# Query projection of a fused attention and feed-forward kernel, as seven half-size products per block instead of eight

## The chip, the cores and the metric

The kernel runs on one core of one Trainium2 chip. The metric is the device time of one launch in microseconds (us). Before the change it is 1665.83 us, the median of 3 runs (1663.76 to 1665.88).

## What is computed

Two layers, each a cross attention and a feed-forward stage, are applied to x of 32 x 64 = 2048 tokens with 512 features. The change is in the first attention, whose reference is:

```
q = (layernorm(x) @ wq).reshape(b, tq, HQ, D)      # HQ = 32 heads of D = 128; wq is 512 x 4096
k = (ctx @ wk).reshape(b, tk, HKV, D)              # HKV = 8; wk, wv are 512 x 1024
v = (ctx @ wv).reshape(b, tk, HKV, D)
scores = einsum('bqhd,bkhd->bhqk', q / sqrt(D), repeat(k, 4))
probs = softmax(scores, axis=-1)                   # 64 x 64 for each head and sequence
x = x + einsum('bhqk,bkhd->bqhd', probs, repeat(v, 4)).reshape(b, tq, HQ * D) @ wo
```

## The kernel before

Every matrix product works on pairs of float16 numbers: an operand is split into a high part (ScalarE casts) and a low part (VectorE subtracts), and three products are summed (high by high, high by low, low by high: `PASSES`).

A first part, the opening, loads x and the context, normalises x (VectorE computes the statistics, GpSimd writes `XN`), transposes both on TensorE and splits them into `XT` and `CT` in units of one PSUM bank. Then `attention0` loops over 8 groups; a group is one key head with its four query heads. Seven of the groups run as a hardware loop and the last is written out. Within a group there are four windows (t = 0 to 3), one for each block of 512 tokens.

TensorE's order in the window of block t is written by hand: scores of block t; the projections of the block after it, four query heads in turn, then the key; weighing of values of block t, pair 0 (it needs `PT`, the transposed probabilities, which come by DMA); the value projection of the next block; pair 1; the output projection of block t in four pieces, added into `X` by VectorE (`accumulate`). Each unit of a projection goes through one of two banks `pj`; ScalarE copies its high part (`high`), VectorE subtracts the low part (`low`), and then the bank is free again.

VectorE and ScalarE each have an order written by hand too. On VectorE: maximum and difference for both halves of the scores (`scores_less_max`), then for each half sums, the low part of a query head, and `normalise`; `low_probs` twice; the remaining low parts; `low_out`; `accumulate`. SyncE issues the DMA transposes of `EH` into `PT` once both high and both low halves are there. The kernel also prepares the fp8 weights of the feed-forward stage beside this: in window 1 and 2 ScalarE scales eight tiles, and in windows 2 and 3 it copies 1024 columns (`high_weights`), while GpSimd has two operations after each of windows 1 and 2, and nothing else in a group. In window 2 both ScalarE and VectorE split the next group's `WQ` and `WKV`, VectorE between the first and second `accumulate`.

## Time and profile before

| what | value |
|---|---|
| median of 3 runs | 1665.83 us (1663.76 to 1665.88) |
| profiled execution, span from first to last instruction | 1663.4 us |
| time outside the span (median less span) | 2.4 us |
| TensorE matmuls | busy 1510.4 us, 91% of the span |
| VectorE | busy 1273.3 us, 77% |
| ScalarE | busy 789.3 us, 47% |
| GpSimd | busy 289.0 us, 17% |
| bytes moved by DMA | 113.48 MB, 68 GB/s on average |

The profile was taken on one execution, and it gives a span only; its own time is taken as the span plus the 2.4 us around it. In the profile PE is TensorE, DVE is VectorE, ACT is ScalarE, POOL is GpSimd, SP is SyncE. Busy shares are averages over the stages; the first attention is the part from 56.8 to about 1011 us.

### The profile page before, as it was taken

To read this page: it belongs to the slowest core of one execution; us is meant where nothing else is said; L and a number is where in the kernel's file an instruction comes from. 1 tells how busy PE (TensorE), PEld (TensorE's weight loads), DVE (VectorE), ACT (ScalarE), POOL (GpSimd) and SP (SyncE) were. 2 spreads that over 40 slices of the span, in tenths; PEclk is the share of its full clock that TensorE was granted. 3 is DMA by queue.
4 is the path that set the end of the run, shared out by engine and by line. 5 is a ranking of instruction groups with operands and counts; after the bars stand their busy time and mean duration, and the time that the engine had idled before them with its cause. 6 is when DMAs were issued, how large, how long until landed. Compare 5 with 4: busy or idle time off the path is not lost. (4 is left out here: it accounts for less than half of the span.)

```text
span 1663.4 us, 29998 instructions
## 1 busy us (share of the span) xinstructions
PE 1510.4 (91%) x11382; PEld 803.7 (48%) x11398; DVE 1273.3 (77%) x2386; ACT 789.3 (47%) x1677; POOL 289.0 (17%) x249
## 2 busy tenths in 40 slices
PE   5799999999999999999999987799999998787695
PEld 4455455555555555555555543344444544344353
DVE  6577667667677667767776786899999986999777
ACT  3343433424334243342333332566777763888652
POOL 2001002001011011011011001111211103789620
PEclk7799999999999999999999998899999999899898
DMA  7031231321312212221312112122222350767402
GB/s 265 1 78 51 68 85 26 79 75 43 98 39 66 76 52 64 68 61 52 77 51 62 48 70 102 23 45 45 45 44 44 58 117 1 140 107 123 79 1 101
DMA packets 273838, 113.48 MB, mean 68 GB/s; under 512 B 239154, under 2 KB 255539, under 8 KB 273460
## 3 DMA queue, kind: packets, MB, share of 16 engines
q1 hardware_dynamic: 234820, 78.67, 21.6%
q10 hardware_dynamic: 38896, 33.03, 6.3%
q8 instruction: 94, 1.54, 0.4%
q14 instruction: 28, 0.23, 0.0%
HBM read 44.57 MB, written 11.53 MB: 34 GB/s over the span
## 5 line engine op out<-in xcount | busy, mean ns | idle before, releaser
L627 PE MATMUL xp<-WO,OT 128*128 128x512 f16 x1536 | 341.1, 382 | 5.6 <-DVE X L824 5.6
L585 PE MATMUL pj<-XT,WQ 128*128 128x512 f16 x1536 | 339.0, 381 | 6.4 <-PEq L379 6.4
L627 PEld LDWEIGHTS xp<-WO,OT 128*128 128x128 f16 x1536 | 148.2, 98 | 189.3 <-issue 18.4
L585 PEld LDWEIGHTS pj<-XT,WQ 128*128 128x128 f16 x1536 | 148.4, 98 | 182.3 <-DVE WKV L294 6.7
L705 ACT ACTIVATE E<-E 128x512 f32<-128x512 f32 x64 | 40.1, 627 | 329.0 <-DVE E L801 329.0
L824 DVE SCALAR_TENSOR_TENSOR X<-xp,X 128x512 f32<-128x512 f32 x128 | 88.2, 690 | 113.0 <-PE xp L627 112.0
L565 POOL TENSOR_TENSOR VW<-VW,XB 128x1024 f32<-128x1024 f32 x14 | 32.9, 2351 | 769.8 <-DVE VW L107 769.8
L1028 PE MATMUL db<-W0T,XD 128*128 128x448 f16 x768 | 162.2, 363 | 0.0
L1045 PE MATMUL eb<-W1T,DT 128*128 128x512 f16 x672 | 147.7, 380 | 4.2 <-ACT EB L1120 2.5
L766 DVE SCALAR_TENSOR_TENSOR QT<-pj,QT 128x512 f16<-128x512 f32 x128 | 88.0, 687 | 67.9 <-ACT QT L688 67.6
L1028 PEld LDWEIGHTS db<-W0T,XD 128*128 128x128 f16 x768 | 76.9, 100 | 74.7 <-issue 8.0
L688 ACT ACTIVATE QT<-pj 128x512 f16<-128x512 f32 x128 | 75.5, 590 | 71.1 <-PE pj L585 71.0
L1100 ACT ACTIVATE VD<-VD,dscale 128x128 f32<-128x128 f32 x224 | 68.7, 390 | 75.1 <-DVE VD L1202 75.1
L1045 PEld LDWEIGHTS eb<-W1T,DT 128*128 128x128 f16 x672 | 65.6, 98 | 78.7 <-DMA DT<-HL 1.1
L775 DVE TENSOR_TENSOR OT<-tv,OT 128x512 f16<-128x512 f32 x128 | 82.3, 684 | 13.8 <-ACT OT L697 11.1
L590 PE MATMUL pj<-WKV,CT 128*128 128x128 f16 x1536 | 91.3, 220 | 0.9 <-DVE QT L766 0.9
L585 PE MATMUL pj<-CT,WKV 128*128 128x512 f16 x384 | 88.2, 380 | 4.0 <-DVE QT L766 4.0
L590 PEld LDWEIGHTS pj<-WKV,CT 128*128 128x128 f16 x1536 | 85.9, 98 | 7.7 <-issue 6.3
L697 ACT ACTIVATE OT<-tv 128x512 f16<-128x512 f32 x128 | 69.3, 593 | 26.2 <-PE tv L616 26.2
L710 ACT ACTIVATE EH<-E 128x512 f16<-128x512 f32 x64 | 40.3, 630 | 84.5 <-DVE E L813 84.5
L1401 POOL TENSOR_TENSOR CT<-CT 128x512 f16<-128x512 f32 x64 | 72.6, 1159 | 16.9 <-ACT CT L1631 16.7
L1093 ACT ACTIVATE VD<-DB,drec 128x128 f32<-128x128 bf16 x224 | 67.2, 387 | 12.3 <-DVE drec L85 12.3
(236 smaller groups left out, 2427.0 us busy)
## 6 DMA issues: line engine op xcount, KB each, us to landing
W0T<-in_L_xattn_wq ACTq DMA_DIRECT2D x7, 1024.0 KB, 5.3
W0T<-in_L_xattn_wo ACTq DMA_DIRECT2D x7, 1024.0 KB, 5.0
CS<-in_ctx SPq DMA_DIRECT2D x4, 1024.0 KB, 10.1
X<-in_x SPq DMA_DIRECT2D x4, 1024.0 KB, 11.2
out<-X SPq DMA_DIRECT2D x8, 512.0 KB, 3.6
XB<-in_L_ffn_W ACTq DMA_DIRECT2D x28, 128.0 KB, 2.8
w0t<-XB ACTq DMA_DIRECT2D x7, 512.0 KB, 3.3
w1t<-W0T ACTq DMA_DIRECT2D x7, 512.0 KB, 3.8
```

Of the source, the lines that this page charges most:

```text
L585: last = pe.matmul(bank[:, :], w, src[:, b, k, tokens], start=n == 0, stop=n == 3 * KC - 1)
L590: last = pe.matmul(bank[:, i * P:(i + 1) * P], CT[:, a, k, own], WKV[:, b, k, 1, :], start=n == 0, stop=n == 3 * KC - 1)
L627: last = pe.matmul(xp[i % 2][:, :], OT[:, a, j, i * P:(i + 1) * P], WO[:, b, j, :], start=n == 0, stop=n == 3 * REP - 1)
L688: act.activation(QT[:, 0, :, u, :], q_bank(u), ACT.Copy, scale=UNSCALE).then_inc(S["pj_hi"], 1)
L697: act.activation(o_out(0, pair, h), o_bank(h), ACT.Copy).then_inc(S["ot_hi"], 1)
L766: dve.scalar_tensor_tensor(out=to[0], in0=q_bank(u), scalar=UNSCALE, in1=to[1], op0=ALU.mult, op1=ALU.subtract).then_inc(S["pj_lo"], 1)
L775: dve.tensor_tensor(o_out(1, pair, h), o_bank(h), o_out(0, pair, h), ALU.subtract).then_inc(S["ot_lo"], 1)
L824: dve.scalar_tensor_tensor(out=xt, in0=xp[i % 2][:, :], scalar=UNSCALE, in1=xt, op0=ALU.mult, op1=ALU.add).then_inc(S["x_acc"], 1)
L1028: last = pe.matmul(db[q][:, 0:NQ], XD[:, i[1] % 2, a, k, :], W0T[:, b, k, q * NQ:(q + 1) * NQ], start=False, stop=n == 3 * KC - 1)
L1045: last = pe.matmul(eb[:, :], DT[:, a, c, :], W1T[:, b, c, :], start=False, stop=c == IC - 1 and (a, b) == PASSES[-1])
L1100: last = act.activation(VD[:, r, c, :], VD[:, r, c, :], ACT.Copy, scale=ds_[:, r, c:c + 1])
L1401: pool.tensor_tensor(EH[:, 1, q, :], E[:, q, :, :].rearrange("p u n -> p (u n)"), EH[:, 0, q, :], ALU.subtract).then_inc(S["e_lo"], 1)
```

## The change

The four query heads of a group are computed for a block by a Strassen scheme (Winograd's form). The 512 tokens are halved, the 512 features are halved, and the four heads are halved. Instead of 8 half-size products, 7 are made: of sums of quarters of the weights by sums of quarters of x. Before, a block's queries took 48 matmuls of 512 columns; now they take 84 of 256 columns.

What goes with it:

- The seven combinations of x are made in the opening: GpSimd subtracts quarters, TensorE transposes 14 chunks for each pair of token tiles where there were 8, and ScalarE and VectorE split them. They are stored in DRAM (`xt7`), and SyncE fetches the next block's 14 KB per partition once its predecessor's products are done and the block's transposes of `PT` have landed (`load_x`).
- The combinations of the weights are made by GpSimd once a group (`sum_q`, four operations of 512 columns, in window 1), and split by five operations on ScalarE and five on VectorE instead of one each (`high_q`, `low_q`).
- The seven products go into four banks, `pj` and `xp`. ScalarE copies two of them out as float32 (`copy_lone`), VectorE adds the other five (`add_products`), and GpSimd makes two sums between them (`add_lone`). ScalarE then rounds the four sums to `QT` (`high_queries`) and GpSimd subtracts the low parts (`low_queries`), which was VectorE's work before.
- On VectorE `normalise` now stands ahead of the operation on queries, and the key projection uses bank `xp[1]`.

The core of the diff:

```diff
+A11, A12, S4, NA22, S1, S2, S3 = range(7)
+B11, B21, B22, T1, T2, T3, T4 = range(7)
+        def sum_q(pool, g):
+            pool.wait_ge(W["sq_ld"], g * 16 + 16)
+            pool.tensor_tensor(as_quarter(S12[:, 0, :]), quarter(1, 0), quarter(1, 1), ALU.add).then_inc(W["wq_sum"], 1)
...
-            act.activation(WQ[:, 0, :, :], SQ[:, :, :], ACT.Copy, scale=WEIGHT_SCALE).then_inc(W["qkv_hi"], 1)
+            act.wait_ge(W["wq_sum"], g * 4 + 4)
+            for first, size, source, sign in Q_SPLITS:
+                act.activation(wq_part(0, first, size), source, ACT.Copy, scale=sign * WEIGHT_SCALE).then_inc(W["q_hi"], 1)
...
+                for q in range(2 * BLOCKS):
+                    a, b, s = XN[:, q % 2, 0, :], XN[:, q % 2, 1, :], TS[:, q % 2, :, :]
...
+                    pool.tensor_tensor(s[:, 0, :], b[:, 0:256], a[:, 0:256], ALU.subtract).then_inc(ts_ready, 1)
+                    pool.tensor_tensor(s[:, 2, :], b[:, 256:512], b[:, 0:256], ALU.subtract).then_inc(ts_ready, 1)
...
+            def load_x(g, t, after):
+                sp.wait_ge(S["qp_done"], n_of(g, t, SEVEN, SEVEN))
...
+                    if g < GROUPS - 1 or t < SPG - 2:
+                        sp.wait_ge(S["pt_done"], n_of(g, t, 32, 32))
+                        load_x(g, t + 1, (t + 2) % SPG)
...
+            def add_lone(g, t):
+
+                pool.wait_ge(S["q_copy"], n_of(g, t, 2, 2))
+                pool.wait_ge(S["q_sum"], n_of(g, t, 5, 1))
+                pool.tensor_tensor(C12[:, :], C21[:, :], C22[:, :], ALU.add).then_inc(S["q_pool"], 1)
+                pool.wait_ge(S["q_sum"], n_of(g, t, 5, 2))
+                pool.wait_ge(S["q_pool"], n_of(g, t, 2, 1))
+                pool.tensor_tensor(C22[:, :], U3[:, :], C22[:, :], ALU.add).then_inc(S["q_pool"], 1)
+
+            def low_queries(g, t):
+                for n, (source, pair, half) in enumerate(QUARTERS):
+                    pool.wait_ge(S["qt_hi"], n_of(g, t, 4, n + 1))
+                    pool.tensor_tensor(q_out(1, pair, half), source[:, :], q_out(0, pair, half), ALU.subtract).then_inc(S["qt_lo"], 1)
...
+            def product(bank, w, xq):
+                for m in range(2):
+                    to = bank[:, :].rearrange("p (b m t) -> p b m t", m=2, t=SEQ)[:, :, m, :]
+                    for n, (k, (a, b)) in enumerate([(k, ab) for ab in PASSES for k in range(2)]):
+                        last = pe.matmul(to, WQ[:, a, w, (2 * k + m) * HEAD0:(2 * k + m + 1) * HEAD0],
+                                         XT[:, b, xq, k, :].rearrange("p (b t) -> p b t", t=SEQ), start=n == 0, stop=n == 5)
...
                     for jp in range(2):
                         sums(g, t, jp)
+                        normalise(g, t, jp)
                         if more:
-                            low(*nxt, jp)
-                        normalise(g, t, jp)
+                            add_products(*nxt, (jp,))
                     low_probs(g, t, 0)
                     low_probs(g, t, 1)
                     if more:
-                        low(*nxt, 2)
+                        add_products(*nxt, (2, 3, 4))
```

How it moves instructions is shown at three places. The first is TensorE in window 1 of a group: `sc` are the scores, `pj` and `xp` the banks. Before:

```order
L599 MATMUL sc<-KT,QT 128x64 x48
L585 MATMUL pj<-XT,WQ 128x512 x12
L579 REGISTER_ALU
L585 MATMUL pj<-XT,WQ 128x512 x12
L579 REGISTER_ALU
L585 MATMUL pj<-XT,WQ 128x512 x12
L579 REGISTER_ALU
L585 MATMUL pj<-XT,WQ 128x512 x12
L579 REGISTER_ALU
L585 MATMUL pj<-CT,WKV 128x512 x12
```

Each register row belongs to a wait on VectorE's low parts. The same place now:

```order
L771 MATMUL sc<-KT,QT 128x64 x48
L724 REGISTER_ALU
L716 MATMUL pj<-XT,WQ 128x4x64 x24
L732 REGISTER_ALU
L716 MATMUL xp<-XT,WQ 128x4x64 x12
L735 REGISTER_ALU
L716 MATMUL xp<-XT,WQ 128x4x64 x12
L738 REGISTER_ALU
L716 MATMUL pj<-XT,WQ 128x4x64 x12
L741 REGISTER_ALU
L716 MATMUL xp<-XT,WQ 128x4x64 x12
L744 REGISTER_ALU
```

Four products start without a wait on this window's softmax; the fifth and sixth wait for the two copies of ScalarE (L738, L741), the seventh for VectorE's first sum (L744).

The second place is VectorE in the same window, from the sums of the first half of the probabilities (`E`) to the low halves `EH`. Before:

```order
L807 TENSOR_REDUCE ST<-E 128x8
L809 RECIPROCAL ST<-ST 128x8
L763 ISA
L766 SCALAR_TENSOR_TENSOR QT<-pj,QT 128x8x64
L813 TENSOR_TENSOR E<-E,ST 128x512
L807 TENSOR_REDUCE ST<-E 128x8
L809 RECIPROCAL ST<-ST 128x8
L763 REGISTER_ALU
L766 SCALAR_TENSOR_TENSOR QT<-pj,QT 128x8x64
L813 TENSOR_TENSOR E<-E,ST 128x512
L818 TENSOR_TENSOR EH<-E,EH 128x512 x2
```

And now, where `C` and `U` are the float32 sums of products:

```order
L1023 RECIPROCAL ST<-ST 128x8
L1027 TENSOR_TENSOR E<-E,ST 128x512
L961 REGISTER_ALU
L963 REGISTER_ALU
L965 REGISTER_ALU
L973 SCALAR_TENSOR_TENSOR C<-pj,C 128x512
L1021 TENSOR_REDUCE ST<-E 128x8
L1023 RECIPROCAL ST<-ST 128x8
L1027 TENSOR_TENSOR E<-E,ST 128x512
L961 REGISTER_ALU
L967 REGISTER_ALU
L973 SCALAR_TENSOR_TENSOR U<-xp,C 128x512
```

The two normalisations have moved ahead of the operations on queries, and the two `EH` operations and three further sums follow.

The third place is GpSimd in window 1 of a group. Before, it had only the two operations on `VW` there; now six stand ahead of them, and then the four of `sum_q` on `W0T` and `S4F`:

```order
L675 TENSOR_TENSOR C<-C 128x512
L676 REGISTER_ALU
L677 REGISTER_ALU
L678 TENSOR_TENSOR C<-U,C 128x512
L682 REGISTER_ALU
L683 TENSOR_TENSOR QT<-C,QT 128x512
L682 REGISTER_ALU
L683 TENSOR_TENSOR QT<-C,QT 128x512
L682 REGISTER_ALU
L683 TENSOR_TENSOR QT<-C,QT 128x512
L682 REGISTER_ALU
L683 TENSOR_TENSOR QT<-C,QT 128x512
```

The first adds two sums once ScalarE's second copy is there, the second follows VectorE's second sum, and the last four follow ScalarE's roundings.

## Rows read from the trace of the kernel before

**Rows 1.** Timeline of TensorE, one group: start us, length us, instructions, idle before.

```profile
193.26 1.57 PE L599 MATMUL sc<-KT,QT 128*128 128x64 f16 x48
...
205.70 2.76 PE L585 MATMUL pj<-CT,WKV 128*128 128x512 f16 x12 [0.50 <-DVE QT L766]
...
223.07 1.56 PE L599 MATMUL sc<-KT,QT 128*128 128x64 f16 x48
224.47 10.52 PE L585 MATMUL pj<-XT,WQ 128*128 128x512 f16 x48
...
237.52 0.83 PE L616 MATMUL tv<-PT,V 64*128 64x256 f16 x12
...
252.20 1.56 PE L599 MATMUL sc<-KT,QT 128*128 128x64 f16 x48
...
271.14 0.83 PE L616 MATMUL tv<-PT,V 64*128 64x256 f16 x12 [0.88 <-DVE OT L775]
...
282.27 1.56 PE L599 MATMUL sc<-KT,QT 128*128 128x64 f16 x48
...
311.44 1.57 PE L599 MATMUL sc<-KT,QT 128*128 128x64 f16 x48
```

**Rows 2.** Timelines of VectorE and ScalarE, window 1 (it starts at 223.07).

```profile
230.67 0.69 DVE L766 SCALAR_TENSOR_TENSOR QT<-pj,QT 128x512 f16<-128x512 f32 x1 [0.35 <-ACT QT L688]
231.28 0.68 DVE L813 TENSOR_TENSOR E<-E,ST 128x512 f32<-128x512 f32 x1
231.87 1.47 DVE L818 TENSOR_TENSOR EH<-E,EH 128x512 f16<-128x512 f32 x2
...
229.52 0.63 ACT L710 ACTIVATE EH<-E 128x512 f16<-128x512 f32 x1 [1.14 <-DVE E L813]
```

**Rows 3.** The DMA transposes of `PT`: issue time in ns, min/median/max, and landing.

```profile
L536 SPq DMA_TRANSPOSE PT<-EH x64: 1232/1307/1857, 84.0 to 998.8; - x64
...
DMA to landing us min/median/max: 2.7/2.8/3.5
```

**Rows 4.** Timelines of GpSimd and VectorE where both work, at 979 and 1100.

```profile
978.82 1.27 POOL L241 TENSOR_TENSOR VW<-VW 128x512 f32<-128x512 f32 x1 [99.23 <-DVE VW L107]
980.17 1.04 POOL L243 TENSOR_TENSOR VW<-VW,xscale 128x512 f32<-128x512 f32 x1
...
979.46 0.65 DVE L167 TENSOR_TENSOR ln_work<-guess 128x4 f32<-128x4 f32 x1
...
980.34 0.90 DVE L169 TENSOR_SCALAR ln_work<-ln_work 128x4 f32<-128x4 f32 x1
...
1095.38 2.08 DVE L107 TENSOR_TENSOR VD<-VD,MD 128x896 f32<-128x896 f32 x2
...
1100.09 2.93 DVE L1202 TENSOR_TENSOR VD<-VD,MD 128x896 f32<-128x896 f32 x2
...
1100.32 1.76 POOL L1277 TENSOR_TENSOR VW<-VW,xscale 128x512 f32<-128x512 f32 x1 [19.00 <-DVE VW L1178]
```

**Rows 5.** Groups of GpSimd's instructions: count, busy us, mean ns of one, idle before.

```profile
L1401 POOL TENSOR_TENSOR CT<-CT 128x512 f16<-128x512 f32 x64 | 72.6, 1159 | 16.9 <-ACT CT L1631 16.7
```

**Rows 6.** Timelines of ScalarE and VectorE, window 2 (it starts at 252.20).

```profile
264.65 2.43 ACT L673 ACTIVATE VW<-XB,wrec 128x128 f32<-128x128 bf16 x8
266.99 1.04 ACT L682 ACTIVATE XB<-VW 128x1024 f16<-128x1024 f32 x1
...
275.31 2.28 DVE L289 SCALAR_TENSOR_TENSOR WQ<-W0T,WQ 128x2048 f16<-128x2048 f32 x1
```

**Rows 7.** The DMA issue of 3.5 MB: count, KB each, median us to landing.

```profile
W1T<-w1t SPq DMA_DIRECT2D x1, 3584.0 KB, 12.6
```

**Rows 8.** Timelines of VectorE and GpSimd in the opening, one block.

```profile
19.69 2.46 DVE L151 BATCH_NORM_STATS2 bn<-X 128x6 f32<-128x512 f32 x4
...
24.18 1.52 POOL L417 TENSOR_SCALAR XN<-X,rstd,nmr 128x512 f32<-128x512 f32 x2 [6.94 <-DVE nmr L174]
...
30.36 2.46 DVE L151 BATCH_NORM_STATS2 bn<-X 128x6 f32<-128x512 f32 x4
```

More of the change, by code:

```diff
@@ L479, in attention0 @@
 def attention0(nc, sb, pb, sem, X, ident, XT, CT, w0, w1, w0t_dram, w1t_dram, ahead_of_ffn0,
[L480 removed]
+               weights, weight_sems, loads, splits, x_store, piece, bits16, VW, first_x, ended):
     exp_scale = float(HEAD0) ** -0.5
@@ L526, in n_of, with q_out @@
             return g * (SPG * per) + (t * per + c)
+        def q_out(part, pair, half):
+            return QT[:, part, half, pair, :]
+        QUARTERS = ((C22, 1, 1), (C11, 0, 0), (C12, 0, 1), (C21, 1, 0))
         @block.sync
@@ new lines, in group @@
+            def group(g, last):
+                for t in range(SPG):
+                    nxt = (g, t + 1) if t < SPG - 1 else (g + 1, 0)
+                    if not last or t < SPG - 1:
+                        add_lone(*nxt)
+                        low_queries(*nxt)
+                    if t == 1 and not last:
+                        sum_q(pool, g + 1)
+                    for p in prepared(t, last):
+                        dequantise_weights(g, *p)
+            add_lone(0, 0)
+            low_queries(0, 0)
@@ new lines, in queries @@
+            def queries(g, t, window):
+                first = window is None
+                if not first:
+                    pe.wait_ge(S["xt_ld"], n_of(g, t, 16, 0))
+                pe.wait_ge(W["q_lo"], g * 5 + 1)
+                product(pj[0], A11, B11)
+                if not first:
+                    pe.wait_ge(S["kv_lo"], n_of(g, t, 2, 0))
+                pe.wait_ge(W["q_lo"], g * 5 + 2)
+                product(pj[1], S2, T2)
+                if not first:
+                    pe.wait_ge(S["x_acc"], n_of(*window, 4, 1))
+                product(xp[0], S1, T1)
+                if not first:
+                    pe.wait_ge(S["x_acc"], n_of(*window, 4, 2))
+                pe.wait_ge(W["q_lo"], g * 5 + 3)
+                product(xp[1], S3, T3)
+                pe.wait_ge(S["q_copy"], n_of(g, t, 2, 1))
+                product(pj[0], A12, B21)
+                pe.wait_ge(W["q_lo"], g * 5 + 4)
+                pe.wait_ge(S["q_copy"], n_of(g, t, 2, 2))
+                product(xp[0], S4, B22)
+                pe.wait_ge(W["q_lo"], g * 5 + 5)
+                pe.wait_ge(S["q_sum"], n_of(g, t, 5, 1))
+                product(pj[1], NA22, T4)
@@ new lines, in project @@
+            def project(g, t, value):
+                tokens = slice(t * BLOCK, (t + 1) * BLOCK)
+                passes = [(k, ab) for ab in PASSES for k in range(KC)]
+                if not value:
+                    pe.wait_ge(W["kvw_lo"], g + 1)
+                    pe.wait_ge(S["q_sum"], n_of(g, t, 5, 2))
+                    for n, (k, (a, b)) in enumerate(passes):
+                        last = pe.matmul(xp[1][:, :], WKV[:, a, k, 0, :], CT[:, b, k, tokens], start=n == 0, stop=n == 3 * KC - 1)
+                else:
+                    pe.wait_ge(S["q_sum"], n_of(g, t, 5, 5))
+                    for i in range(BT):
+                        for n, (k, (a, b)) in enumerate(passes):
+                            own = slice(t * BLOCK + i * P, t * BLOCK + (i + 1) * P)
+                            last = pe.matmul(pj[1][:, i * P:(i + 1) * P], CT[:, a, k, own], WKV[:, b, k, 1, :],
+                                             start=n == 0, stop=n == 3 * KC - 1)
+                last.then_inc(S["kv_done"], 1)
@@ L646, in group @@
                         scores(g, SPG - 1)
-                    project_out(g, t)
+                    project_out(g, t, nxt if more else None)
             pe.sem_inc(S["xp_done"], 1)
-            project(0, 0, range(6))
+            pe.sem_inc(S["x_acc"], 2)
+            queries(0, 0, None)
+            project(0, 0, False)
+            project(0, 0, True)
             with pe.Fori(0, GROUPS - 1) as g:
@@ L717, in group @@
                     if more:
-                        high(*nxt, range(2, 4))
+                        high_queries(*nxt)
                     for p in prepared(t, last):
@@ L754, in _ @@
             act.sem_inc(S["w_st"], 16)
-            high(0, 0, range(6))
+            copy_lone(0, 0, 0)
+            copy_lone(0, 0, 1)
+            high_queries(0, 0)
+            high_key(0, 0)
+            high_value(0, 0)
+            act.wait_ge(xt_st[3], 16)
             with act.Fori(0, GROUPS - 1) as g:
@@ L884, in group @@
                         first_x[1](dve)
-                    if more:
-                        low(*nxt, 3)
                     x_ahead(1)
@@ L914, in group @@
                             low_kv(dve, g + 1)
-            for u in range(6):
-                low(0, 0, u)
+            add_products(0, 0, range(5))
+            low_key(0, 0)
+            low_value(0, 0)
             with dve.Fori(0, GROUPS - 1) as g:
```

308 lines of the change are left out of this document (197 added, 111 removed).

## The prediction

> **What bounds the kernel now.** I read the timeline of TensorE over one group first, since the change lies in the loop of the first attention. Scores start at 193.26, 223.07, 252.20, 282.27 and 311.44 [rows 1]: windows 0 to 3 take 29.81, 29.13, 30.07 and 29.17 us, a group 118.2 us. TensorE waits 0.50 in window 0 and 0.88 in window 2 and hardly elsewhere, so it is the bound, but a thin one. Beside it run two chains with nearly its length. The first is the softmax: in window 1 the low halves of the probabilities end at 233.34, which is 10.27 after the window's start [rows 2]; a DMA transpose takes 1.3 us to issue and lands 2.8 us after its start [rows 3]; the second is issued at about 10.85 and lands at 13.65, and values are weighed from 14.45 (237.52) [rows 1]. That leaves 0.8 us. The second is ScalarE's row of copies in window 2, which already delays the second weighing by 0.88 us [rows 1].
>
> **What the products save.** The 48 matmuls of 512 columns take 10.52 us, 0.219 us each [rows 1]. No row shows this shape with 256 columns; I take half of it, 0.110 us, since it is the same stream of columns. 84 of them take 9.24 us against 10.4, a saving of 1.12 us a window. The upper bound is that half the columns save nothing on the fixed part, say 0.12 us each: then only 0.3 us is saved. With that a window without any wait takes 29.12 - 1.12 = 28.0 us.
>
> **What GpSimd costs VectorE.** This is the term that decides. GpSimd gets six operations of 512 columns in each window, and the like cost 1.16 us in one row [rows 5] and 1.27 in another [rows 4]; I take 1.2. Rows 4 show what such an operation does to VectorE. GpSimd works from 978.82 to 980.09 and from 980.17 to 981.21. VectorE's tiny operation at 979.46 (four columns, normally under 0.2 us) ends at 980.11, and that of 980.34 at 981.24: each ends when GpSimd's does. At 1100.09 a pair of 896 columns takes 2.93 us where the same shape takes 2.08 at 1095.38, and GpSimd's operation from 1100.32 takes 1.76. So VectorE's operations with two inputs in SBUF, and its tensor_scalar, don't share with GpSimd: the one that comes second waits for the whole of the other. That agrees with the Trainium skill, page "SBUF — State Buffer", section "Who interferes with whom", which says that a VectorE instruction with two SBUF inputs contends with a GpSimd instruction that reads SBUF, and that the loser blocks fully. By a fair sharing of the port the rows at 1100 could be read too (0.85 us lost over 2.7 us of overlap); that is a rival below.
>
> Of VectorE's operations in a window, both normalisations and both low halves `EH` have two SBUF inputs; the five sums of products have one in PSUM. I lay the orders of the change side by side, window 1, times from its start:
>
> - First normalisation 5.3 to 5.95; ScalarE's high half 6.0 (6.45 before [rows 2], since an operation on queries stood ahead); its second copy 6.5 to 7.1; so GpSimd's first sum runs 7.2 to 8.4.
> - The second normalisation started at 8.21 before [rows 2]. It now comes 0.8 earlier (0.35 of waiting and an operation of 0.6 are no longer ahead of it, 0.1 is waited for the reciprocal), at 7.4. It meets GpSimd's sum and ends at 8.95 instead of 8.1.
> - VectorE's second sum ends at 9.55. The first `EH` is issued at 9.5, just ahead of GpSimd's second sum (9.6), and ends at 10.2; GpSimd then runs to 11.4; the second `EH` waits for it and ends at 12.0.
> - The second transpose is issued at 12.05 and lands at 14.9. TensorE is there at 1.40 + 9.24 + 2.69 = 13.33 and **waits 1.6 us**.
>
> In window 0 VectorE starts 0.75 us earlier and the wait is 0.85. In windows 2 and 3 the first normalisation meets GpSimd's work on the weights as well, and it is 2.4 in each.
>
> **ScalarE's chain.** The last rounding of queries now needs VectorE's fifth sum, which stands behind both `EH` operations. In window 1 that sum ends at 13.85, the rounding at 14.4; then come 2.3 of scaling, the key and two output copies (0.5 each), and two operations of VectorE: 19.2, against TensorE at 14.95 + 0.76 + 2.79 = 18.5. It **waits 0.8**. In window 2 the rounding ends at 15.35, the scaling and the 1024-column copy end at 18.65 [rows 6], and VectorE's second output operation at 21.8, against 19.45: **2.4 us**. In windows 0 and 3 it is 0.1 to 0.2, and the copy for the sixth product costs 0.15 in two windows.
>
> **The split of the weights.** VectorE's one operation of 2.28 us between the first and second `accumulate` [rows 6] becomes two of 1.14 and three of 0.6, 4.1 us. TensorE's fourth output piece needs the second `accumulate`; before, that was 0.9 early, now it is **1.05 late**. ScalarE's five operations there lie in its idle time.
>
> **Sum of the loop.** Waits are 1.0, 2.4, 5.9 and 2.8 us in the four windows: 4 x 28.0 + 12.1 = 124.1 to 124.2 us a group against 118.2, +6.0, and 42 us in seven groups. In the last group VectorE also normalises x ahead of the next stage, work that holds tiny operations and tensor_scalar, so windows 1 and 2 suffer more, and nothing is split: I take +7.
>
> **The opening.** A block took 30.36 - 19.69 = 10.67 us [rows 8]. GpSimd wrote two tiles in 1.52 us; now it makes four subtractions of 256 columns behind each two tiles, at half of 1.16 [rows 5] and 0.07 between, 2.6 us. Statistics take 4.5 us (to 24.18), two pairs 8.2, and the last unit needs 1.5 more: 14.2 us, +3.5, in four blocks +14. Five splits instead of one and GpSimd's sums beside the statistics add 2. If GpSimd ran ahead unnoticed, VectorE's eight units (two of them short) alone would make it 11 us a block, +1.5 in all; if its subtractions cost 0.8 each, +19. I take +16.
>
> **DMA.** A block's x is 1.8 MB, half of the transfer that lands in 12.6 us [rows 7], so some 6 to 7 us. It is issued when `PT` has landed, at 15, and lands by 22; the next products start at 29. The work that hides it is the output projection; without that cover it would cost up to 7 us a window. The weight transposes behind it on SP's queue are needed only a window later. I cost it at nothing.
>
> **Total.** 1663.4 + 16 + 42 + 7 = 1728 us of span; with the 2.4 us around it 1731, and the profiled execution's own time stands for the median of 1665.8. The run is 3.9% slower.
>
> **The rivals.**
>
> - Sharing instead of blocking. If VectorE and GpSimd each lost about a third of the time in which they overlap, the same chains give 119.8 us a group, +11 in seven, +3 in the last: 1696. For it: 0.85 of 2.7 us at 1100. Against it: the two tiny operations that end with GpSimd's. The middle between the two also stands for VectorE winning most of the races for second place.
> - No meeting at all: if GpSimd's sums fell into gaps of VectorE, the group is 115.8 us. Window 2 still gains nothing, since ScalarE's row and the split of the weights stand; the loop gives 17 us back and the opening takes 16: 1665. Against it: the first sum follows the copy that follows the high half, so it starts beside the second normalisation by its own chain.
> - Faster: TensorE stays the bound in every window. It needs one thing, that the transposes and output halves are always early, as if the VectorE chain were 2.4 us shorter. Then a group is 112 us, -43 in seven and -4 in the last, and with the opening the run takes 1634. It decides from about 2.3 us of waiting in a group: under this the kernel gains. Against it: TensorE had only 0.8 us of room in window 1 and none in window 2, and 1.12 of the room goes with the saving itself.
> - Worse: the x fetch or a weight transpose comes late as well, or the halves cost 0.12 us a matmul with TensorE's clock dropping in the waits: over 1750.
>
> **How the numbers follow.** Blocking 0.70 (1715 to 1750), sharing or half of the races 0.14 (1685 to 1715), no meeting 0.06 (1660 to 1685), faster 0.04, worse 0.06. The prediction is 1731. The range leaves out the last three mostly and takes in the bounds of GpSimd's price and the opening: 1688 to 1752. A measurement of this kernel can tell about 0.2% from no change, which is 3.3 us: faster 0.06, the same 0.04, slower 0.90.
>
> **What would show it.** In the new trace: groups of about 124 us; product matmuls at 0.110 us each; VectorE's second normalisation and second `EH` over 1.2 us where they took 0.7; TensorE's wait for `PT` in every window, 0.9 to 2.4 us, and for `OT` of 2.4 us in window 2; a wait for `X` of about 1 us in window 2; blocks of 14 us in the opening; x landing before 23 us of a window. The prediction is wrong if those VectorE operations keep their 0.7 us, or if the waits for `PT` are missing.

## The result

Before 1665.86 us (median of 4 runs), after 1779.29 us (1774.68 to 1781.68, 4 runs): ratio 1.068, 95% interval 1.0663 to 1.0696. The change makes the kernel 6.8% slower; 1731 was forecast, within 1688 to 1752. The direction holds, the size doesn't: 113 us measured against 65.

The page of the changed kernel, its head and the groups that matter:

```profile
span 1776.9 us, 33608 instructions
...
PE 1528.1 (86%) x12582; PEld 947.4 (53%) x12598; DVE 1380.6 (78%) x2466; ACT 847.5 (48%) x1789; POOL 609.7 (34%) x505
...
L675 POOL TENSOR_TENSOR C<-C 128x512 f32<-128x512 f32 x32 | 41.2, 1288 | 397.0 <-ACT C L862 397.0
L683 POOL TENSOR_TENSOR QT<-C,QT 128x512 f16<-128x512 f32 x128 | 168.4, 1339 | 23.7 <-ACT QT L870 23.7
...
L788 PE MATMUL tv<-PT,V 64*128 64x256 f16 x768 | 59.1, 292 | 78.6 <-DMA PT<-EH 44.6
```

The weighing of values (`tv`) now has 78.6 us of idle time ahead of it, most of it until `PT` lands. The timeline of TensorE, from window 2 of the loop's first group to the start of the next group's window 0, answers to [rows 1]; pieces that only multiply are left out:

```profile
170.55 1.12 PE L788 MATMUL tv<-PT,V 64*128 64x256 f16 x12 [2.20 <-DMA PT<-EH]
171.60 4.15 PE L761 MATMUL pj<-WKV,CT 128*128 128x128 f16 x48
176.61 0.83 PE L788 MATMUL tv<-PT,V 64*128 64x256 f16 x12 [0.85 <-DVE OT L989]
...
186.28 2.75 PE L801 MATMUL xp<-WO,OT 128*128 128x512 f16 x12 [0.97 <-DVE X L1038]
...
188.87 1.56 PE L771 MATMUL sc<-KT,QT 128*128 128x64 f16 x48
190.27 2.79 PE L716 MATMUL pj<-XT,WQ 128*128 128x256 f16 x24
192.89 2.78 PE L716 MATMUL xp<-XT,WQ 128*128 128x256 f16 x24
...
204.65 1.08 PE L788 MATMUL tv<-PT,V 64*128 64x256 f16 x12 [2.22 <-DMA PT<-EH]
205.66 4.19 PE L761 MATMUL pj<-WKV,CT 128*128 128x128 f16 x48
...
222.50 0.41 PE L771 MATMUL sc<-KT,QT 128*128 128x64 f16 x8 [1.42 <-issue]
225.54 2.29 PE L771 MATMUL sc<-KT,QT 128*128 128x64 f16 x40 [2.63 <-issue]
227.65 3.43 PE L716 MATMUL pj<-XT,WQ 128*128 128x256 f16 x24
```

Three things are to be seen. The forecast waits are there: 2.2 us for `PT`, 0.85 for `OT`, 0.97 for `X`. After the 2.2 us the value projection takes 4.15 to 4.19 us where it took 2.85 before. And where the loop jumps back to window 0, two waits stand that no engine and no transfer of data ends: 1.42 us ahead of the scores, and 2.63 us behind the first 8 of their 48 matmuls. "Issue" means that TensorE waited for nothing that the profile shows.

By the starts of scores, and with the forecast beside them (means over the seven passes of the loop): window 0 takes 32.55 us (29.0 forecast), window 1 30.2 (30.4), window 2 34.8 (33.9), window 3 33.3 (30.8). The 113.5 us of longer span are 19.5 until the first scores of the loop (94.12 against 74.58 before), 87.7 in the loop's seven passes and 6.2 behind it; forecast were 16, 42 and 7. So 46 of the 48 missing microseconds lie in the loop, in windows 0 and 3 above all.

### The profile page after: what moved, and what is told of

It is laid out like the page before. It is cut to its first block and busy times, and to the rows that moved or that the text cites. A ratio compares the mean times of both kernels' runs of the same rounds, so it can differ in the third digit from the quotient of the medians.

```text
span 1776.9 us, 33608 instructions
## 1 busy us (share of the span) xinstructions
PE 1528.1 (86%) x12582; PEld 947.4 (53%) x12598; DVE 1380.6 (78%) x2466; ACT 847.5 (48%) x1789; POOL 609.7 (34%) x505
## 5 line engine op out<-in xcount | busy, mean ns | idle before, releaser
L716 PE MATMUL pj<-XT,WQ 128*128 128x256 f16 x1536 | 191.3, 280 | 7.6 <-PEq L419 7.4
L675 POOL TENSOR_TENSOR C<-C 128x512 f32<-128x512 f32 x32 | 41.2, 1288 | 397.0 <-ACT C L862 397.0
L683 POOL TENSOR_TENSOR QT<-C,QT 128x512 f16<-128x512 f32 x128 | 168.4, 1339 | 23.7 <-ACT QT L870 23.7
L716 PE MATMUL xp<-XT,WQ 128*128 128x256 f16 x1152 | 136.4, 273 | 0.9
L788 PE MATMUL tv<-PT,V 64*128 64x256 f16 x768 | 59.1, 292 | 78.6 <-DMA PT<-EH 44.6
L716 PEld LDWEIGHTS xp<-XT,WQ 128*128 128x128 f16 x1152 | 111.6, 98 | 17.7 <-ACT C L862 4.8
L870 ACT ACTIVATE QT<-C 128x512 f16<-128x512 f32 x128 | 78.5, 630 | 60.6 <-POOL C L678 43.6
L761 PE MATMUL pj<-WKV,CT 128*128 128x128 f16 x1536 | 106.2, 237 | 0.0
L761 PEld LDWEIGHTS pj<-WKV,CT 128*128 128x128 f16 x1536 | 100.8, 108 | 8.0 <-issue 7.7
L688 POOL TENSOR_TENSOR VW<-VW,XB 128x1024 f32<-128x1024 f32 x14 | 32.9, 2351 | 209.5 <-DVE VW L115 209.5
L1493 POOL TENSOR_TENSOR VW<-VW,xscale 128x512 f32<-128x512 f32 x15 | 24.6, 1642 | 230.6 <-DVE VW L1394 221.0
```

Of the source, the lines that this page charges most:

```text
L675: pool.tensor_tensor(C12[:, :], C21[:, :], C22[:, :], ALU.add).then_inc(S["q_pool"], 1)
L683: pool.tensor_tensor(q_out(1, pair, half), source[:, :], q_out(0, pair, half), ALU.subtract).then_inc(S["qt_lo"], 1)
L716: last = pe.matmul(to, WQ[:, a, w, (2 * k + m) * HEAD0:(2 * k + m + 1) * HEAD0], XT[:, b, xq, k, :].rearrange("p (b t) -> p b t", t=SEQ), ...
L761: last = pe.matmul(pj[1][:, i * P:(i + 1) * P], CT[:, a, k, own], WKV[:, b, k, 1, :], start=n == 0, stop=n == 3 * KC - 1)
L788: last = pe.matmul(tv[h][:, s * 256:(s + 1) * 256], V[rows, t % 2, a, 2 * pair + s, :], PT[rows, b, :, 2 * pair + s, :], start=n == 0, sto ...
L870: act.activation(q_out(0, pair, half), source[:, :], ACT.Copy).then_inc(S["qt_hi"], 1)
```

## The experiments

Theory A, the prediction's: VectorE's operations with two SBUF inputs stand still for the whole of a GpSimd operation. Theory B, formed on the rows above: TensorE's instructions come in blocks by DMA, the jump's target now lies near the end of a block, and the fetch of the target itself waits for other transfers. Against B stands C: the waits at the jump come with the longer loop body, whatever its place. The expectations speak of seven groups for the jump; a loop of seven passes jumps back six times, so their sums are a seventh too large.

### 1. The place of the loop in its block of instructions

```
             project(0, 0, True)
+            for _ in range(32):
+                pe.matmul(sc[0][:, 0:8], WKV[:, 0, 0, 0, :], CT[:, 0, 0, 0:8], start=True, stop=True)
             with pe.Fori(0, GROUPS - 1) as g:
```

> Edit: 32 tiny matmuls (8 columns, into a score bank that is free then) ahead of TensorE's loop; nothing else. They cost some 2 us once. The theory under test: TensorE's instructions come in blocks by DMA, and the loop's first instruction now lies so near the end of a block that only 8 of the 48 score matmuls are in the block that the jump fetches; the next block is asked for only then, and takes the 2.4 to 2.6 us that stand as issue waits before the other 40. By it the shift takes that second wait away in seven groups (17.5 us) and with it perhaps 1 us a group of TensorE at its lower clock: 1752 to 1763 us. Rival: the waits come from the longer loop body or from the transfers at the end of a group; then the shift changes nothing, 1779 to 1783 us, and both waits stand as before.

Measured: 1757.43 us, ratio to before 1.0553 (1.0535 to 1.057), 22 us less than the changed kernel, by 32 useless matmuls. TensorE's timeline at the first jump:

```profile
222.80 1.57 PE L771 MATMUL sc<-KT,QT 128*128 128x64 f16 x48 [0.84 <-issue]
224.21 2.79 PE L716 MATMUL pj<-XT,WQ 128*128 128x256 f16 x24
```

The second wait is gone, and scores and products behind it run at full speed: 1.57 and 2.79 us, where the 40 scores took 2.29 and the products 3.43. Over the six jumps the 22 us are 3.6 us each. In the windows 0 that follow a jump the mean falls from 32.9 to 30.0 us, and the rest is a shorter first wait: 0.26 to 0.84 us, where it was 0.77 to 1.65.

The same thing with the opposite sign, in the kernel before the change: 84 such matmuls ahead of its loop.

> Edit: the kernel before the change, with 84 tiny matmuls (8 columns) ahead of TensorE's loop, so that the loop's first instruction stands at the same place of its block of 256 instructions as in the changed kernel. They cost some 5 us once. The theory of the instruction blocks: a wait of 2.4 to 2.6 us behind the first 8 or so score matmuls in each of seven groups, and up to 1 us more at the lower clock: 1666 + 5 + 17 to 24 = 1688 to 1695 us. Rival (the waits at the loop's end come from the changed body, its length or its transfers): 1671 us, with no issue wait.

Measured: 1688.27 us, ratio 1.0139 (1.0122 to 1.0156). Its timeline at the first jump:

```profile
194.82 0.72 PE L599 MATMUL sc<-KT,QT 128*128 128x64 f16 x19
198.03 1.02 PE L599 MATMUL sc<-KT,QT 128*128 128x64 f16 x29 [2.49 <-issue]
```

A kernel without one issue wait gets one of 1.9 to 2.5 us at each jump, with its loop body untouched. It comes behind 19 of the 48 matmuls and not behind 8, so the place was not hit exactly. So the wait belongs to the place, not to the body: C falls for this part. In the profiled execution the tiny matmuls take 2.1 us and not the 5 expected, the seven passes are 19.2 us longer than before, which is 3.2 us a jump, and some 5 us lie behind the loop, which this run does not explain.

The transfers show the blocks. First the kernel before, in slices of 0.25 us from 186 us, then the changed one, from 216 us; the digits are the busy share of the DMA engines in tenths, GB/s what they moved:

```profile
DMA  9999800000000000030000000000000300000000
GB/s 412 401 393 401 336 0 0 0 0 0 0 0 0 0 0 0 0 66 0 0 0 0 0 0 0 0 0 0 0 0 0 66 0 0 0 0 0 0 0 0
...
q8 instruction: 2, 0.03, 1.6%
```

```profile
DMA  0000099999999999200010000002000000000000
GB/s 0 0 0 0 10 301 346 354 344 348 350 453 401 385 393 451 66 0 0 8 16 8 25 0 0 0 0 66 0 0 0 0 0 0 0 0 0 0 0 0
...
q8 instruction: 2, 0.03, 1.3%
```

Each 66 is one packet of instructions, 16 KB: 66 GB/s for 0.25 us. Before, one comes at 190.2 us, 3 us ahead of the scores at 193.26, and the next at 193.7, when the block is entered; both are in time. After, the first comes at 220.0, in the slice in which the 1 MB of the stores ends, and scores start 2.5 us later; the next comes at 222.8, when the 8 matmuls have run, and again 2.7 us pass. The Trainium skill, page "Runtime: NRT & Kernel Launch", section "Instruction fetch mechanics", says that instructions are fetched in blocks of 256 (16 KiB), the next one while one is executed, and that a taken jump out of the window forces a fetch before execution goes on. The trace agrees, and adds the price here: in both kernels TensorE starts its scores 2.5 to 3.25 us behind the first packet at each jump, and a wait of 1.9 to 2.9 us stands when the target has few instructions left in its block, none when it has many and no transfer is in the way.

### 2. No jump at all

The four loops over groups are written out (`with pe.Fori(...) as g` becomes `for g in range(...)`, and so on ScalarE, VectorE and GpSimd).

> Edit: the loop over seven groups written out on PE, ScalarE, VectorE and GpSimd, so that no engine jumps back. The theory (the jump finds its target's instructions not yet fetched): both issue waits go in all seven groups (4.0 us each) and some 1.5 us of lower clock behind them: 28.8 us for window 0 as in the last group, 1738 to 1750 us. Rival (the instructions' transfers are held up by the other transfers, wherever they come): waits of the same kind at other places of the group, 1765 us or more.

Measured: 1743.1 us, ratio 1.0462 (1.044 to 1.0484), 36 us less. No issue wait is left at a group's start; window 0 takes 29.2 us behind the first group (once 29.8), windows 1, 2 and 3 are 30.1, 34.0 and 30.6 to 32.1. The six passes behind the first take 123.9 to 126.0 us, 125.0 in the mean, against 124.2 forecast. So with the jump taken out, the forecast of the loop was right to about 1 us a group. The jumps of all four engines went here at once; that TensorE's is the one that counts rests on section 1.

### 3. The first wait and the stores

```
-                    if g < GROUPS - 1 or t < SPG - 2:
-                        sp.wait_ge(S["pt_done"], n_of(g, t, 32, 32))
-                        load_x(g, t + 1, (t + 2) % SPG)
                     for n, lo, hi in prepared(t - 1, g == GROUPS - 1):
...
+                        sp.wait_ge(S["wt_done"], g * 64 + n * 32 + 32)
+                    if g < GROUPS - 1 or t < SPG - 2:
+                        sp.wait_ge(S["pt_done"], n_of(g, t, 32, 32))
+                        load_x(g, t + 1, (t + 2) % SPG)
```

> Edit: SyncE issues the two transposes of the FFN weights ahead of the fetch of the next x block in windows 2 and 3 (and waits for them to land first), so that the weights' stores are issued right after the transposes instead of 10 us later. The theory: the first issue wait at the loop's end (0.8 to 1.65 us) is the fetch of the loop's first instructions held up by the two stores of 0.5 MB; without them it is gone, 7 x 1.2 = 8 us less, 1768 to 1773 us; the second wait (2.4 to 2.6) stands. Rival: the first wait has nothing to do with the stores: no change from that, 1779; and if the x fetch then lands after window 3's end, a wait of TensorE for XT and a slower kernel, over 1785 us.

Measured: 1781.12 us (1.0672 to 1.0708), no change, and the first wait stands, 0.98 to 3.69 us. This looked like the end of the idea that the stores cause it. It was not: the stores were issued 5 us earlier (210.63 instead of 215.90), but now ran beside the 1.8 MB of the x fetch, and their landing took 8.1 us or more instead of 3.3 to 5.7. At the first jump the traffic still ended at about 219.8 us; in the passes with the waits of 3.6 and 3.7 us it ended later than TensorE was due. The edit had moved the issue and not the end. So another one, that puts the stores behind the jump:

```
                     if t == SPG - 1 and not last:
+                        act.wait_ge(S["sc_done"], n_of(g, SPG, 2, 1))
                         store_weights(act, g)
```

> Edit: the changed kernel, in which ScalarE waits for the first scores of the next group before it issues the two stores of the prepared weights (0.5 MB each); nothing else. In the run with the weights' transposes first the stores were issued earlier but shared the DMA engines with the x fetch, so that the traffic still ended just ahead of the jump. The theory: the first issue wait at the loop's end (0.8 to 1.65 us, 0.5 to 0.8 with 32 matmuls ahead) is the fetch of the loop's first instructions, which starts only when the traffic of the stores has drained; with the stores behind the jump it is gone: 7 x 1.2 = 8 us less, 1771 us (1766 to 1774), and the second wait stands at 2.4 to 2.6 us or grows, as the stores now meet that fetch (then 1775 to 1785 us, with a first wait of nearly zero). Rival: the first wait has another cause and stands at 0.8 to 1.65 us, 1779 us.

Measured: 1782.0 us (1.0666 to 1.0705). The jump, on TensorE:

```profile
221.50 0.40 PE L771 MATMUL sc<-KT,QT 128*128 128x64 f16 x8
224.29 1.33 PE L771 MATMUL sc<-KT,QT 128*128 128x64 f16 x40 [2.38 <-issue]
```

The first wait is gone (0 to 0.23 us at the jumps read), and the second alone is left. The theory of the stores stands. The time doesn't fall, and that is a new wait, not a rival's victory: on ScalarE the two issues, from 225.08, and the table load behind them, end at 228.7, so the first exponential starts at 228.71 in this window, the probabilities are late, and TensorE waits 2.2 us for `PT` in window 0, which in the changed kernel was 0.7 us at most behind a jump.

The instruction packets tell what sets the length of the first wait. In the changed kernel the first packet comes 2.9 to 4.3 us behind the issue of the first store, between 1.0 us ahead of the end of the stores' traffic and 0.5 behind it, and the scores are due 4.9 to 5.4 us after that issue. With 32 matmuls ahead the packet comes about as far behind the issue, 3.9 to 4.2 us, but the scores are due 6.0 to 6.5 us after it: hence the shorter waits of 0.26 to 0.84 us. In the run of section 4 the first store is issued only 3.7 to 4.2 us ahead of the due scores; there the packet of the first jump, at 210.3 us, is ahead of the bulk of the stores' traffic, and the first waits are 0 to 0.43 us with the stores in their place.

### 4. GpSimd's sums without their size

```
-                pool.tensor_tensor(C12[:, :], C21[:, :], C22[:, :], ALU.add).then_inc(S["q_pool"], 1)
+                pool.tensor_tensor(C12[:, some], C21[:, some], C22[:, some], ALU.add).then_inc(S["q_pool"], 1)
```

`some` is 8 columns in the loop, and the same in the second sum and the four subtractions. So this kernel leaves out the rest of these sums and low halves, and its output is not the reference's.

> Edit: in the loop, GpSimd's two sums and four subtractions of the query projection work on 8 columns instead of 512 (the rest of those queries is left out, so the output is not the reference's); all waits and signals stay. The theory of the prediction (VectorE's operations stand still while a GpSimd operation with two inputs runs): the waits for PT (1.3, 2.2, 2.2 us) and OT go, with them the V projections at half clock; windows of 28.0 to 29.5 us instead of 30.2, 34.1, 33.0; a group of 119 to 121 us with the waits at the loop's end still there, against 131 now: 1695 to 1710 us. Rival (the new order of VectorE's work or the wait for ScalarE sets PT's time, and GpSimd only shares): PT waits of over 1 us stay in windows 2 and 3, 1740 us or more.

Measured: 1713.86 us, ratio 1.030 (1.026 to 1.034), 65 us less than the changed kernel, though 4 us above the range. The waits for `PT` fall from 1.3, 2.2 and 2.2 us to none, 0.39 and 0.38, window 1 takes 28.15 us, and the value projection 2.85 again. What the expectation left out is window 2, at 33.7: there a wait for `OT` of 2.2 us (ScalarE's chain through the weights' row) and that for `X` of 0.97 stand untouched by GpSimd. Window 0 stays at 32.3 us in the mean behind a jump, against 28.6 in the first pass: the jump costs 3.7 us where no other wait overlaps it.

That the operations meet is seen in the changed kernel itself, window 1; VectorE first, then GpSimd:

```profile
129.71 0.69 DVE L1027 TENSOR_TENSOR E<-E,ST 128x512 f32<-128x512 f32 x1
...
131.87 1.65 DVE L1027 TENSOR_TENSOR E<-E,ST 128x512 f32<-128x512 f32 x1
133.45 0.68 DVE L973 SCALAR_TENSOR_TENSOR U<-xp,C 128x512 f32<-128x512 f32 x1
134.05 2.35 DVE L1032 TENSOR_TENSOR EH<-E,EH 128x512 f16<-128x512 f32 x2
136.32 0.68 DVE L973 SCALAR_TENSOR_TENSOR C<-pj,C 128x512 f32<-128x512 f32 x1
...
137.52 0.67 DVE L973 SCALAR_TENSOR_TENSOR C<-pj,U 128x512 f32<-128x512 f32 x1
...
131.71 1.27 POOL L675 TENSOR_TENSOR C<-C 128x512 f32<-128x512 f32 x1 [19.07 <-ACT C L862]
134.28 1.57 POOL L678 TENSOR_TENSOR C<-U,C 128x512 f32<-128x512 f32 x1 [1.31 <-DVE U L973]
136.59 4.53 POOL L683 TENSOR_TENSOR QT<-C,QT 128x512 f16<-128x512 f32 x4 [0.74 <-ACT QT L870]
```

The same normalisation takes 0.69 us alone and 1.65 beside GpSimd's sum: from 132.98, where that ends, it needs 0.54 more. The two halves `EH` take 2.35 instead of 1.47 [rows 2]. But the three sums with an input in PSUM keep 0.67 to 0.68 us under GpSimd's subtractions.

The same by itself, in the kernel before the change: one addition of 1024 columns on GpSimd in each window, on a tile that nobody reads, released by the second reciprocal.

```
+              for tt in range(SPG):
+                pool.wait_ge(S["rcp_done"], n_of(g, tt, 2, 2))
+                pool.wait_ge(dummy, n_of(g, tt, 1, 1))
+                pool.tensor_tensor(DUMMY[:, :], DUMMY[:, :], DUMMY[:, :], ALU.add).then_inc(dummy, 1)
```

> Edit: the kernel before the change, with one GpSimd addition of 1024 columns (two SBUF inputs, a scratch tile that nobody reads, some 2.1 us) in each window of the loop, released by the second reciprocal, so that it meets VectorE's second normalisation. Nothing else of the kernel changes. Theory (VectorE's operation stands still until GpSimd's is done): the normalisation takes 1.9 us or more instead of 0.68, PT comes 1.2 to 1.4 us later, against a slack of 0.8 in window 1 and less in windows 2 and 3: some 2 to 3 us a group, 1680 to 1690 us. Rival (they share the port): 0.3 us later at most, within the slack: 1666 to 1669 us.

Measured: 1677.72 us, ratio 1.0075 (1.0058 to 1.0092). VectorE, then GpSimd, in window 1:

```profile
231.22 0.68 DVE L823 TENSOR_TENSOR E<-E,ST 128x512 f32<-128x512 f32 x1
...
233.69 1.64 DVE L823 TENSOR_TENSOR E<-E,ST 128x512 f32<-128x512 f32 x1
...
232.90 1.89 POOL L569 TENSOR_TENSOR DUMMY<-DUMMY 128x1024 f16<-128x1024 f16 x1 [29.06 <-DVE ST L819]
```

GpSimd's operation ends at 234.79 and the normalisation at 235.33, again 0.54 later. It lost 0.96 us of an overlap of 1.10, and ended a fixed 0.54 behind: it stood still until GpSimd's was done, theory A. Sharing, by the prediction's third of the overlap, would have cost it 0.4 us. The time is below the 1680 expected, since GpSimd took 1.89 us and not 2.1, so that the normalisation lost 0.96 instead of 1.2. A pass is 1.9 us longer: 0.9 in window 0, 0.8 in window 3, 0.25 in window 1, where most falls into the slack of 0.8, and nothing in window 2.

### 5. Taking the waits out

On the written-out loop, GpSimd's two sums go to VectorE, behind the low halves `EH`; its four subtractions stay.

```
+            def add_lone(g, t):
+                dve.wait_ge(S["q_copy"], n_of(g, t, 2, 2))
+                dve.wait_ge(S["q_sum"], n_of(g, t, 5, 2))
+                dve.tensor_tensor(C12[:, :], C21[:, :], C22[:, :], ALU.add).then_inc(S["q_pool"], 1)
...
                     if more:
+                        add_lone(*nxt)
                         add_products(*nxt, (2, 3, 4))
...
```

> Edit: on the written-out loop of the run before (1743 us), the two sums of the query projection that GpSimd made (C12 and C22) go to VectorE, behind the low halves of the exponentials; GpSimd keeps its four subtractions. The theory: only GpSimd's two sums meet VectorE's operations with two SBUF inputs ahead of PT; its subtractions meet operations that read PSUM, which do not stand still. By it the PT waits of 1.3, 2.2 and 2.2 us fall to 0.4 or less, as with 8 columns, window 1 takes 28.2 us, and a group some 120 instead of 126: 1743 - 7.5 x 6 = 1698 us (1690 to 1710). Rival: GpSimd's four subtractions (1.3 us each) hold VectorE up too; then PT or OT waits of over 1 us stay in windows 1 and 3: 1720 us or more.

Measured: 1746.09 us (1736.95 to 1751.96), ratio 1.0483 (1.044 to 1.0526): no gain over 1743, and my number was off by 48 us. The `PT` waits did go (0 to 0.4 us is left in the loop, but for one of 1.3 and one of 1.85), so the half of the theory on who meets whom holds. But longer waits for `OT` took their place, mostly 1.5 to 3.5 us: against the written-out kernel, windows 1 and 3 fell by 0.6 and 1.2 us in the mean, and windows 0 and 2 rose by 1.3 and 1.2. ScalarE in window 1:

```profile
261.22 2.43 ACT L859 ACTIVATE QT<-C 128x512 f16<-128x512 f32 x4 [2.50 <-DVE C L970]
263.55 2.43 ACT L835 ACTIVATE VW<-XB,wrec 128x128 f32<-128x128 bf16 x8
265.89 0.57 ACT L863 ACTIVATE KT<-xp 128x512 f16<-128x512 f32 x1
```

ScalarE idles 2.50 us until VectorE has made `C22`, then does the queries, then 2.43 us of the weights' row, and only then the key and the output halves, for which TensorE waits at 268.44. The chain by way of ScalarE was as long as the one by way of `PT`, within a microsecond; with one out of the way the other decides.

The next kernel moves the weights' row and high half out of window 2's chain, spreads VectorE's five splits of the query weights over the four accumulates, and takes the moments of a block in the opening ahead of the low halves of the block before:

```
+                        if t == SPG - 2 and not last:
+                            low_q(dve, g + 1, ((0,), (1,), (2, 3), (4,))[i])
                         if i == 0:
-                            if t == SPG - 2 and not last:
-                                low_q(dve, g + 1)
...
-                    if n % PER_BLOCK == 0:
-                        ln_stats_vector(dve, 0, (n // PER_BLOCK,), x_ld)
+                    if n == 0:
+                        ln_stats_vector(dve, 0, (0,), x_ld)
+                    if n % PER_BLOCK == BT and n // PER_BLOCK < BLOCKS - 1:
+                        ln_stats_vector(dve, 0, (n // PER_BLOCK + 1,), x_ld)
...
```

> Edit: the kernel of the run above, with three changes of order. In window 2 the ScalarE row of 2.43 us goes to the end of window 1, the high half of the weights behind the value's copy, the low half on VectorE behind the value's; the five splits of the query weights on VectorE are spread over the four accumulates instead of standing in a row behind the first. In the opening, each block's moments are taken ahead of the low halves of the block before. Expected: window 2 falls from 34 to 29 to 31 us (VectorE then has nearly 30 us of work in it), 7 x 4 = 28 us; the opening's period falls from 15.4 to 12.3 us, as GpSimd's 6.5 us of idle time goes, some 9 us: 1698 - 37 = 1661 us, against 1666 of the kernel before the change. Rival for window 2: the wait is VectorE's sum of work, which reordering cannot take away: 33 us and 1685 us.

Measured: 1691.16 us, ratio 1.0169 (1.0144 to 1.0194). Its parts came in: window 2 takes 28.7 us instead of 33.4 to 36, and the loop's first scores start at 83.74 instead of 93.02. The sum was too low by 30 us: it started from the 1698 that the run beside it did not reach, 48 too low, and its parts gave 55 us where 37 were expected, nearly all of the surplus in window 2, which fell by 6.4 us a pass instead of 4.

The last one changes ScalarE's order alone (the same lines are taken out where they stood):

```
+                    if t == 0 and not last:
+                        load_weights(act, g)
                     for jp in range(2):
                         act.wait_ge(S["sub_done"], n_of(g, t, 2, jp + 1))
...
-                        if more and jp == 0:
-                            copy_lone(*nxt, 0)
+                        if more:
+                            copy_lone(*nxt, jp)
...
                     for p in prepared(t, last):
                         if t == 1:
                             weights_times_rec(g, *p)
+                    if more:
+                        high_queries(*nxt)
...
```

> Edit: the kernel with the new orders (1691 us), with four moves on ScalarE: the weights' row of window 1 (2.43 us) into the 2.5 us in which it waits for C22, ahead of the queries' high halves; the four loads of FFN weights of window 0, which held ScalarE's queue for 3.2 us ahead of the key's copy, to the window's start, where it has 10 us of idle time; the copy of the fifth product ahead of the exponentials' high half. The theory: ScalarE's chain is what ends last in windows 0, 1 and 3 now; by it the waits for OT (1.8 and 1.5 us) and for C22 (1.7) go, a group takes 114 to 115 us instead of 118.6, and the kernel 1660 us (1655 to 1672), against 1665 before the change. Rival: VectorE is the next in the chain, so half of each wait stays: 1675 us or more.

Measured: 1661.09 us (12 runs), ratio to the kernel before the change 0.998, 0.9971 to 0.999. Five of the seven passes take 114.83 us, against 118.1 to 118.3 in the steady passes before. TensorE from window 0's scores on:

```profile
200.21 1.56 PE L765 MATMUL sc<-KT,QT 128*128 128x64 f16 x48
...
213.46 0.83 PE L782 MATMUL tv<-PT,V 64*128 64x256 f16 x12
214.23 2.85 PE L755 MATMUL pj<-WKV,CT 128*128 128x128 f16 x48
217.01 0.83 PE L782 MATMUL tv<-PT,V 64*128 64x256 f16 x12
217.77 10.53 PE L795 MATMUL xp<-WO,OT 128*128 128x512 f16 x48
228.14 1.04 PE L765 MATMUL sc<-KT,QT 128*128 128x64 f16 x30
```

Not one wait: 27.93 us, which is the 28.0 that the prediction gave for a window without waits. Windows 2 and 3 (28.7 and 30.2) still wait 0.7 and 1.4 us for `PT`. So the seven products do save: 1.2 us in a window that has no wait either way (29.13 before). Over the seven passes this kernel is 20.4 us shorter than the one before the change, 2.9 us a pass; the opening takes 8.6 us of it back and what stands behind the loop 7.2: 0.2% in all. How much of the 20.4 is the products' and how much the new orders' isn't shown, since no run gave these orders to the kernel before.

## Why the prediction was right in direction and wrong in size

**What bounds the kernel, and the products.** Right. The halves take 0.109 us each (24 of them between the starts at 190.27 and 192.89); window 1 took 30.18 us against 30.4.

**What GpSimd costs VectorE.** Right in mechanism, shown by the runs with 8 columns and with the scratch additions. GpSimd's operations took 1.29 and 1.34 us where I took 1.2; the waits for `PT` were 1.3, 2.2 and 2.2 us in windows 1 to 3 against 1.6, 2.4 and 2.4.

**ScalarE's chain and the split of the weights.** The wait for `X` was 0.97 against 1.05, that for `OT` in window 1 0.83 against 0.8. In window 0 it was 0.2 to 1.2 us where I took 0.1 to 0.2. For `OT` in window 2 it was 2.44 in some passes (2.4 forecast), but 0.85 in others: where the value projection ran in part at the lower clock, as at 171.60 (4.15 us), it used up the wait. In the passes with 2.44 the projection kept its 2.85 us and the clock fell behind that wait instead: window 2 then took 35.7 us instead of 34.1.

**Sum of the loop.** This is the step that failed: "124.1 to 124.2 us a group", as the four windows' waits and nothing else. The mean pass was 130.8. With the jumps taken out (section 2) the loop is 38 us shorter, of the 46 that were missing; the other 8 stand there in window 3 (31.65 us against 30.8), where the clock falls, and in window 0 (29.5 against 29.0). The sum left out three things.

- The jump. I compared instructions on each engine and did not ask where the loop's first one lies in its block. The second wait, with the clock behind it, costs 2.9 us a jump here, where part of it takes the place of other waits, and 3.2 and 3.7 us in the two kernels where it doesn't (sections 1 and 4). Together with a first wait that is 0.6 us longer than in the padded kernel it is 22 us in six jumps.
- The x fetch, "I cost it at nothing". TensorE waits for `XT` only once, 0.21 us, so the transfer itself is hidden, as forecast, though it lands at 23.7 us of window 3 and not at 22. But it delays the weights' transposes behind it on the queue, with these the stores, and the stores end where the jump fetches its instructions. That is the first wait, 0.8 to 1.65 us at each jump (section 3); I had written that the transposes "are needed only a window later".
- TensorE's clock. Before, it was granted in full all through a group. After the waits of 2.2 us for `PT` in windows 2 and 3 the value projection takes 0.9 to 1.6 us longer in 11 of 14 windows, and after those of 1.3 us in window 1 never. From 200 us on:

```profile
core 0: us, PE busy (x) PEld busy (x) DVE busy (x) ACT busy (x) POOL busy (x), PEclk, DMA share, GB/s
...
200.00:205.00 5.00, 2.78 (x20) 1.20 (x19) 3.64 (x5) 3.15 (x5) 4.26 (x4) 1.00 0.47 105
205.00:210.00 5.00, 5.00 (x62) 4.46 (x58) 3.05 (x4) 1.93 (x5) 2.55 (x2) 0.66 0.98 290
```

The mean granted clock of 0.66 from 205 to 210 us is a mixture of the two levels, 1.2 and 2.4 GHz. Every fall that was read in the loop follows a wait of 2 us or more, though not every such wait is followed by one; with `PT` waits of 0.4 us the projection took 2.85 us in every run read. I had the clock in the rival "worse" alone, at 0.06. Window 3 has this and the first wait, which ends it in six passes of seven: 30.8 + 1.4 + 1.1 gives 33.3, as measured. That the wait brings the fall is read from this order of events; no run changed the clock alone.

**The opening.** 19.5 us until the first scores against 16. A block took 15.43 us instead of 14.2, between these two:

```profile
24.66 2.46 DVE L159 BATCH_NORM_STATS2 bn<-X 128x6 f32<-128x512 f32 x4
...
40.09 1.27 DVE L159 BATCH_NORM_STATS2 bn<-X 128x6 f32<-128x512 f32 x2
...
29.14 1.52 POOL L475 TENSOR_SCALAR XN<-X,rstd,nmr 128x512 f32<-128x512 f32 x2 [6.46 <-DVE nmr L182]
30.75 0.72 POOL L477 TENSOR_TENSOR VW<-XN 128x256 f32<-128x256 f32 x1
```

A GpSimd subtraction of 256 columns takes 0.72 us, not half of the 512-column one (0.58): eight of them a block, 1.1 of the 1.2 us. I had named this bound ("+19").

**The last group.** 6.2 us behind the loop against 7.

**The rivals.** Sharing is refuted by the scratch additions. "No meeting" was worked out as 115.8 us a group; the written-out loop with shortened chains reached 114.83. The measured time lies where "worse" was put, but of its terms only the clock came in: the x came in time and the halves took 0.109 us. And the 2.3 us of waiting at which "faster" was said to turn doesn't follow from its own terms: 43 us in seven groups and 4 in the last, less 16 for the opening, leave 31 us over eight groups, 3.9 us each.

## What to carry to other kernels

Before costing a change to a loop's body, ask where the loop's first instruction falls in the stream and what is being transferred when the engine jumps; a few dozen idle instructions ahead of a loop, or writing it out, tells in one run. Where three chains end within a microsecond of each other, a saving on the bound is worth nothing until all of them are shortened, and an edit to one shows nothing by itself: here the first repair on the written-out loop gave 0, and three together 82 us, 10 of them in the opening. A wait costs more than its length if the engine comes back at the lower clock. When an edit that should remove a cause changes nothing, check in the trace that it removed it.

## What was unexpected in the hardware

- 32 tiny matmuls ahead of a loop made the kernel 22 us faster, and 84 made the other one 23 us slower.
- Work resumed 2.5 to 3.25 us behind a packet of 16 KB of instructions on a quiet DMA system. With 1 MB of stores in front, the packet came only in the last microsecond of their traffic or behind it; in two passes, with the x fetch beside them, the wait was 3.6 and 3.7 us.
- VectorE's operation loses 0.96 us of an overlap of 1.1 with GpSimd's (1.64 and 1.65 us for 0.68 and 0.69) if both inputs are in SBUF, and nothing if one is in PSUM.
- The first wait is set by a microsecond in the lead of the stores: issued 4.9 to 5.4 us ahead of the due scores they cost 0.77 to 1.65 us, at 6.0 to 6.5 us 0.26 to 0.84, and at 3.7 to 4.2 us next to nothing. In the kernel before, where they run 10 us ahead and with nothing beside them, they cost nothing. Why the lead differs between the changed kernel and the one with 32 matmuls ahead stays open.
